# Two expert stages of a four-layer transformer kernel: blocks of 256 sorted tokens in place of 512

## The reference

```python
logits = tokens @ Wr + br
expert = jnp.argmax(softmax(logits), axis=-1)
h = relu(einsum('td,edh->teh', tokens, W1) + b1)   # 128 -> 256, of the token's own expert
y = einsum('teh,ehd->ted', h, W2) + b2             # 256 -> 128
out = y[expert] * max_prob
```

## Time and profile before

| what | value |
|---|---|
| median of 3 runs | 2353.3 us (2352.86 to 2362.51) |
| the profiled execution, its span from first to last instruction | 2305.9 us |
| busy in that span: PE, DVE, ACT, POOL | 1971.4, 1503.3, 1078.3, 803.4 us |
| stage b, from the first x issue to the last store | 628.6 to 753.9 us |
| stage d, the same | 2034.3 to 2179.7 us |

### The profile page before, as it was taken

One profiled execution on the slowest core, in us unless ns is written; L12 is line 12 of the kernel. 1 busy time (PEld: TensorE's weight loads), 2 busy tenths in 40 slices (PEclk: granted clock), 3 DMA queues, 4 the chain that ended last, 5 costly groups with the idle time before them and its releaser, 6 DMA issues. The chain is left out here.

```text
span 2305.9 us, 49153 instructions
## 1 busy us (share of the span) xinstructions
PE 1971.4 (85%) x15436; PEld 1024.4 (44%) x15436; DVE 1503.3 (65%) x4596; ACT 1078.3 (47%) x2723; POOL 803.4 (35%) x811
## 2 busy tenths in 40 slices
PE   8477787787388499999999999999999999769896
PEld 6255565565356133334333433343333333346554
DVE  6277888888411577777767867786678777333277
ACT  3356556555134045555545555555455555422221
POOL 4457888888400302221222122212221220100066
PEclk9799999999699599999999999999999999979998
DMA  3452332222187222322132312221322222134333
GB/s 112 155 192 101 108 107 100 88 89 100 49 225 229 89 77 75 101 84 95 63 98 83 97 62 97 84 98 61 98 88 93 74 74 79 52 119 166 133 97 98
DMA packets 127738, 235.73 MB, mean 102 GB/s; under 512 B 17622, under 2 KB 45286, under 8 KB 126966
## 3 DMA queue, kind: packets, MB, share of 16 engines
q1 hardware_dynamic: 118440, 208.51, 27.3%
q0 software_dynamic: 9072, 24.41, 3.7%
HBM read 185.88 MB, written 121.95 MB: 134 GB/s over the span
## 5 line engine op out<-in xcount | busy, mean ns | idle before, releaser
L1622 ACT ACTIVATE c_pT<-c_u 128x512 f32<-128x512 f32 x1024 | 574.5, 596 | 552.0 <-PE c_u L1429 552.0
L1777 DVE CUSTOM_DVE_ANT_0 c_sums<-c_s,bias 128x512 f32<-128x512 f32 x1024 | 665.1, 687 | 254.4 <-PE c_s L1411 229.6
L1411 PE MATMUL c_s<-c_kst,c_qst 126*128 126x512 bf16 x1024 | 320.3, 390 | 16.7 <-issue 12.3
L1429 PE MATMUL c_u<-spread_line,c_pick 128*32 128x512 bf16 x4096 | 316.2, 386 | 0.0
L1443 PE MATMUL c_o<-c_pT,c_vst 128*32 128x256 f32 x4096 | 310.7, 380 | 0.6 <-ACT c_pT L1622 0.5
L1421 PE MATMUL c_u<-c_qst,c_kst 128*128 128x512 bf16 x1024 | 307.5, 381 | 0.2 <-ACT c_pT L1622 0.2
L523 ACT ACTIVATE v<-a_bank,gain 128x64 f32<-128x64 f32 x768 | 165.7, 345 | 53.1 <-DVE vp L737 53.1
L1367 POOL DMA_INDIRECT zs_d<-c_xs,c_slot x64 | 63.2, 988 | 328.0 <-DMA zs_d<-in_zeros 200.6
L1443 PEld LDWEIGHTS c_o<-c_pT,c_vst 128*32 128x32 f32 x4096 | 123.0, 110 | 106.9 <-ACT c_pT L1622 4.0
L389 PE MATMUL a_bank<-wv,xT 128*128 128x512 f32 x256 | 148.9, 667 | 21.1 <-ACT v L523 15.3
L590 POOL TENSOR_TENSOR q<-q,vp 128x1024 f32<-128x1024 f32 x48 | 125.0, 2604 | 100.4 <-DVE vp L737 99.5
(11 more groups left out here) (265 smaller groups left out, 2838.4 us busy)
## 6 DMA issues: line engine op xcount, KB each, us to landing
xs_d<-in_zeros SPq DMA_DIRECT2D x16, 2048.0 KB
zs_d<-in_zeros SPq DMA_DIRECT2D x16, 2048.0 KB, 10.1
c_kst<-parts_d SPq DMA_DIRECT2D x192, 96.0 KB
c_qst<-parts_d SPq DMA_DIRECT2D x192, 96.0 KB
parts_d<-c_parts SPq DMA_DIRECT2D x32, 384.0 KB, 2.5
d_w<-in_wd SPq DMA_DIRECT2D x24, 384.0 KB, 3.2
b_w<-in_wb SPq DMA_DIRECT2D x24, 321.0 KB, 4.7
bias_d<-line_d SPq DMA_DIRECT2D x16, 448.0 KB
```

The source lines that it names most:

```text
L1411: nc.tensor.matmul(s_ps[bank_of(n)][:], qst[0:ROWS_MAX, h, t * P:(t + 1) * P], kst[0:ROWS_MAX, h, :], start=True, stop=True).then_inc(sem( ...
L1429: mm = nc.tensor.matmul(u_ps[bank_of(n)][ARRAY * k:ARRAY * (k + 1), :].rearrange("k (t q) -> k t q", t=T), pick[:], line[:, G * j + i, T - ...
L1622: nc.scalar.activation(pT[n // G % 2][:, n % G, :], u_ps[bank_of(n)][:], ACT.Exp).then_inc(sem("exp_done"), 1)
L1777: v.tensor_tensor_reduce(sums[n % 2][:], s_ps[bank_of(n)][:], bias, 1.0, -3.0e38, ALU.add, ALU.max, top_s[j % 2][:, k:k + 1]).then_inc(sem ...
```

## The change

`GROUP`, the rows of a block, becomes 256 (`BT = 2` sub-blocks of 128), and with it `BLOCKS` becomes 40. Tiles of x, xT, gate, h and y shrink to half; those of w stay. The matmuls of the hidden columns have 256 columns in place of 512; there are 2 transposes and 4 output matmuls in a block in place of 4 and 8. `clear_rows` keeps its pieces of 512 rows, now written with N. A region of the sorted table shrinks from 8704 to 8448 rows. `spread_line` issues a transfer with every second block in place of every block. The loop of four steps makes 9 turns in place of 5. Of the diff, the lines that change:

```diff
@@ -32,7 +32,8 @@
-GROUP = T * P
+BT = 2
+GROUP = BT * P
@@ -171,12 +172,13 @@
-    eng.dma_start(regions[:, bass.ds(GROUP * b, GROUP), :].rearrange("e (p t) w -> p e (t w)", t=T),
+    eng.dma_start(regions[:, bass.ds(N * b, N), :].rearrange("e (p t) w -> p e (t w)", t=T),
...
-    eng.dma_start(io[name][bass.ds(SPARE, GROUP), :].rearrange("(p t) w -> p (t w)", t=T), io["zeros"]).then_inc(done, 16)
+    eng.dma_start(io[name][bass.ds(SPARE, GROUP), :].rearrange("(p t) w -> p (t w)", t=BT),
+                  io["zeros"][:, 0:BT * W]).then_inc(done, 16)
@@ -864,9 +866,9 @@
-        bank = [ctx.enter_context(nc.psum_tensor(f"{tag}_bank{i}", [P, GROUP], F32)) for i in range(8)]
-        turn_ps, gate_ps, h_ps = bank[0:2], bank[2:4], bank[4:6]
-        y_ps = [b[:].rearrange("p (t w) -> p t w", t=T) for b in bank[6:8]]
+        bank = [ctx.enter_context(nc.psum_tensor(f"{tag}_bank{i}", [P, N], F32)) for i in range(8)]
+        turn_ps, gate_ps, h_ps = ([b[:, 0:GROUP] for b in bank[k:k + 2]] for k in (0, 2, 4))
+        y_ps = [b[:, 0:GROUP].rearrange("p (t w) -> p t w", t=BT) for b in bank[6:8]]
@@ -885,12 +887,12 @@
-        x = [sb(f"x{i}", [P, T, W]) for i in range(4)]
+        x = [sb(f"x{i}", [P, BT, W]) for i in range(4)]
...
-        h = [sb(f"h{i}", [P, CHUNKS, T, P]) for i in range(2)]
-        y = [sb(f"y{i}", [P, T, W]) for i in range(4)]
+        h = [sb(f"h{i}", [P, CHUNKS, BT, P]) for i in range(2)]
+        y = [sb(f"y{i}", [P, BT, W]) for i in range(4)]
@@ -906,7 +908,7 @@
-            return io[name][bass.ds(first, GROUP), :].rearrange("(p t) w -> p t w", t=T)
+            return io[name][bass.ds(first, GROUP), :].rearrange("(p t) w -> p t w", t=BT)
@@ -930,7 +932,7 @@
-                    pool.wait_ge(sem("y_ps"), PIECES * k + a + 1)
+                    pool.wait_ge(sem("y_ps"), T // BT * (PIECES * k + a + 1))
@@ -1040,7 +1042,7 @@
-                            v.tensor_tensor(h[b.par % 2][:, c].rearrange("p t n -> p (t n)"), h_ps[c][:], gate[c][:], ALU.mult
+                            v.tensor_tensor(h[b.par % 2][:, c].rearrange("p t n -> p (t n)"), h_ps[c], gate[c][:], ALU.mult
@@ -1049,7 +1051,7 @@
-                            v.tensor_tensor(y[b.par][:], y_ps[b.par % 2], w[b.par][:, ALL - W:ALL].unsqueeze(1).to_broadcast([P, T, W]),
+                            v.tensor_tensor(y[b.par][:], y_ps[b.par % 2], w[b.par][:, ALL - W:ALL].unsqueeze(1).to_broadcast([P, BT, W]),
@@ -1060,18 +1062,18 @@
-                        nc.scalar.copy(xT[s.par % 2][:], turn_ps[s.par % 2][:]).then_inc(sem("xT_ready"), 1)
+                        nc.scalar.copy(xT[s.par % 2][:], turn_ps[s.par % 2]).then_inc(sem("xT_ready"), 1)
...
-                                nc.scalar.activation(gate[c][:], gate_ps[c][:], ACT.Silu).then_inc(sem("gate_ready"), 1)
+                                nc.scalar.activation(gate[c][:], gate_ps[c], ACT.Silu).then_inc(sem("gate_ready"), 1)
...
-                                nc.scalar.activation(h[b.par % 2][:, c].rearrange("p t n -> p (t n)"), h_ps[c][:], ACT.Relu,
+                                nc.scalar.activation(h[b.par % 2][:, c].rearrange("p t n -> p (t n)"), h_ps[c], ACT.Relu,
@@ -1082,14 +1084,14 @@
-                        mm = nc.tensor.matmul(ps[c][:], w[b.par][:, f:f + P], xT[b.par % 2][:], start=True, stop=True)
+                        mm = nc.tensor.matmul(ps[c], w[b.par][:, f:f + P], xT[b.par % 2][:], start=True, stop=True)
...
-                        for t in range(T):
+                        for t in range(BT):
```

## The result

The changed kernel takes 2402.0 us in the median of 4 runs (2394.38 to 2408.38) against 2356.7 for the kernel before. The ratio is 1.019, with a 95% interval of 1.016 to 1.023: 45 us slower. Forecast were 21 us slower, 2374, in a range of 2348 to 2394. The direction was right, the size forecast was under half of the measured one, and the time lies outside of the range.

A forecast was written before the change was run, and what follows sets the result against it. The prediction took TensorE to bound stage d, SP close behind, and the smaller blocks to make SP the bound in both expert stages: +30 us in b and -9 in d, added to 2353.3, gave 2374 us, range 2348 to 2394.

The forecast's parts named there:

- SP's 3.27 us: Both expert stages: average step of the sync engine's queue, a floor whatever the block size, taken as the new bound.
- Rival A: Both expert stages: work stays the bound, d at TensorE's 2.83 us a step; faster, 2319 us; chance 0.1.
- TensorE's busy share in d: Sign for the forecast in the second expert stage: TensorE busy about 85%, idle ahead of each block's transposes.
- Stage d: Second expert stage: bound moves from TensorE to SP, 3.3 us a step; -9 us, bounds -25 and +5.
- The second loop, through y and the landing: Stage d: hidden chunk, store, next x, landing; 6.2 us over two steps, 3.1 each, or 3.3 with a turn.
- Stage b: First expert stage, with the spreading transfers: SP becomes the bound; +30 us, bounds +15 and +45.
- the stretched issues: Stage b: SP issues lengthened by spreading transfers; 19 of the earlier 22.3 us kept under lighter traffic, bounds 4 and 26.
- the register loads: Stage b: the row's load is slower under traffic, 505 ns in the median against 362; 3 us over the stage.
- Rival B: Stage b: SP is the bound but stretches mostly vanish; b +15, d -9, 2359 us, no change; chance 0.2.
- What follows the stage: Stages after an expert stage: start when its last store has landed, no instruction count changes; nothing added, bounds -1 and +2.
- rival C: Stage b: waits drop TensorE to half clock, floor 3.6 us, 14 us more, 2388; chance 0.2, shared with d's 3.7 step.
- 47.4 us lie around the span: Whole kernel: difference between the profiled span of 2305.9 us and the runs' median of 2353.3, taken to stay.

The follow-up runs named there:

- e_static_plan: Changed kernel without SP's register loads in both expert stages (expert and rows constant, routing left out): 2342.2 us, ratio 1.005 to the kernel before.
- e_d_pool: Kernel before with blocks of 256 in stage d only (512 in b) and d's stores issued by GpSimd: 2316.5 us, ratio 0.994.
- e_before_again: The kernel before, unchanged, profiled a second time: 2324.7 us, ratio 1.0004.
- e_after_pad: Changed kernel plus 40 tiny matmuls (160 instructions) ahead of TensorE's first block in stage b: 2360.7 us, ratio 1.015 to the kernel before.
- e_both_off256: Changed kernel with 8704-row regions, stores issued by ScalarE in stage b and GpSimd in d: 2393.3 us, ratio 1.009 to the kernel before.
- e_both_off: Kernel before with blocks of 256 in stage d only, stores issued by ScalarE in b and GpSimd in d: 2351.4 us, ratio 0.990.
- e_no_spread: Changed kernel with stage b's 16 spreading transfers replaced by one memset (position bias left out): 2339.3 us, ratio 1.006 to the kernel before.

## Why the prediction was right and wrong

**Which engine sets the step: right.** SP's 3.27 us was read off a step that waited for nothing, and the steps came out at 3.27 in d, and at 3.28 in b without the spreading. The experiments that make SP's step shorter (e_static_plan, e_d_pool) make d shorter. Rival A is out: the step of d stayed at SP's 3.27 us until SP was relieved, and then fell to 2.97. Of the signs named, TensorE's busy share in d came out at 94% and not about 85%; its own step is 2.97 us and not 2.83, which explains a part (2.97/3.27 is 91%).

**Stage d: right.** -8.2 us against -9. x(4) came 11.95 us behind x(0) (forecast 11.5: 2046.3, less x(0) at 2034.3 and the 0.5 allowed for the plan), the last x 114.5 us later (forecast 115.5), the last store 10.9 us behind it and not 8.7. The second loop, through y and the landing, costs next to nothing beside SP's step in d.

**Stage b: the mechanism right, one term mis-sized.** x(4) stands 10.2 us behind x(0) where 11.0 was forecast (640.1, less 628.6 and 0.5). The 35 steps take 147.7, forecast 136.5; less the stretched issues that is 115.7 against 117.5, and the register loads did not become slower (318 ns in the median; the 3 us allowed for them were not needed). The tail is 8.7 against 7.8. The stretched issues were taken at 19 us with an upper bound of 26, and are 32.0. The argument was that lighter traffic would shorten them. A stretched issue did not get shorter, 32.0/21 = 1.5 us against 22.3/14 = 1.6, and there are more of them: every one of the 16 transfers now stretches an issue and five stretch two (743.15 and 745.35 above), where in the first profile of the kernel before two stretched none and no transfer two. A part of that is chance of the profile that was read, since e_before_again has 18 with 26.4 us. That SP issues more often, and no longer stands in a wait when a transfer starts, is the likely reason and is not tested by itself. Rival B is out with it.

**What follows the stage: wrong, and not seen.** "The other edits ... change no instruction's count, and what follows a stage starts when its last store has landed. I put nothing on them; bounds -1 and +2" is the step that failed: no term of the sum stands for attention_two. The smaller block does change the number of instructions in TensorE's list: 2 transposes and 4 output matmuls fewer in each of the 8 written-out steps that hold them (four of the 8 are the loop's body). A transpose is one weight load and one matmul instruction, and not two matmuls as for the others; an output matmul is two of each. That is 8 x (2 x 2 + 4 x 4) = 160 instructions less ahead of attention_two. With it the turns of attention_two's loop cost some 4 us more each, 14 to 16 us over four where sequences take 74.3 us. e_after_pad shows it by putting 160 back. Where they take 77.6 us, as in the result's own profile, the difference between 256 and 512 in b is 10 us (e_both_off256 against e_both_off). The forecast had named the sign of this, "if attention_two or the last stage moves by over 3 us, the sum has left out a term", and had no term for it, since it looked at stage boundaries for time alone.

**The sum.** +21 forecast; 11 more in b (13 by stretched issues, -2 by the rest), 1 more in d, and 10 to 16 more in attention_two: 43 to 49, measured 45. The kernel before was not profiled on the result's chip, so the last term cannot be given closer there.

**The clock (rival C)** is there in part: b's mean granted clock fell from 0.94 to 0.87. It is not what costs the time, since b's steps less their stretches are (147.7 - 32.0)/35 = 3.31 us, and SP waits for y only 1.0 us from x(4) to the last x. In its reading of the earlier trace rows the 1.92 us, a duration, stands against 0.86, a distance between starts; at the full clock such a pair lasts 1.02. That is a little under twice as long and still the low level. And a floor of 3.6 us against 3.27 makes (3.6 - 3.27) x 35 = 12 us and not 14.

**The baseline.** "47.4 us lie around the span" was wrong too. It did no harm to the sum, which was added to the median, but a span that far under its runs says that it is from another occasion than they are, and the stages should be compared with a second profile.

## What to carry to other kernels

Look for a step in which the issuing queue waits for nothing, and take its length as a price for each block that the block size does not lower: halving the blocks halves the work of TensorE, not the two register loads and three issues of SP. Where a queue is so near to being the bound, move an issue to an idle engine before changing the size: stage d gained 8 us from the smaller blocks and 10 more from the stores on GpSimd. Once the queue has slack, ask what bounds the stage next: in stage b it was the landing under the second load, and less came back than the queue's own sum promised. And after any change to unrolled code look at the loops behind it, for idle time put down to "issue" at their turns.

## What the runs showed of the hardware

- After a transfer of 448 KB issued by GpSimd, one or two of the next issues on SP's queue took 0.8 to 2.8 us in place of 0.35 (changed kernel, 21 issues). No issue of stage b did without such transfers (e_no_spread). Sixteen of them cost 30 to 32 us where SP is the bound. With the stores taken off SP's queue ten of 16 transfers stretched none of its issues (e_both_off), and with SP in a wait the stretches were shorter, 10.4 us over 17 (e_static_plan). Why they stretch an issue is not shown.
- At the four turns of attention_two's loop TensorE stood still for 2.6 to 3.9 us without waiting for any semaphore, and the granted clock was then at its low level for up to 10.2 us (none at one turn). Whether a second wait of 1.1 to 2.8 us follows depended on 160 instructions earlier in its list.
- Two register loads and their arithmetic cost some 1.3 us of a step: store to x 1.95 to 2.02 us with them, 0.73 without.
- The same program took 1296.7 and 1336.8 us in attention_two on two occasions, at a full granted clock between the turns, with expert stages equal to 2 us.
